# Layer norms in an attention and mixture-of-experts kernel: centring and scaling in one VectorE instruction, the mean copied to single precision by GpSimd

## The reference

```python
def _layernorm(x, axis=-1, eps=1e-05):
    m = jnp.mean(x, axis=axis, keepdims=True)
    v = jnp.var(x, axis=axis, keepdims=True)
    return (x - m) / jnp.sqrt(v + eps)
...
x = x + _layernorm(_L0_attn_ref(_layernorm(x), wq, bq, wk, bk, wv, bv, wo, bo))
x = x + _layernorm(_L0_ffn_ref(_layernorm(x), Ws, bs, Wg, Wu, Wd))
```

## Time and profile before

| what | value |
|---|---|
| median of 3 runs | 1080.92 us (1080.68 to 1082.11) |
| the profiled execution | 1085.77 us, span of the instructions 1084.0 us |
| TensorE busy | 839.0 us (77% of the span) |
| VectorE busy | 687.1 us (63%), 2640 instructions |
| ScalarE busy | 555.2 us (51%) |
| GpSimd busy | 367.8 us (34%), 427 instructions |
| mean granted TensorE clock | 0.695 of full speed |

### The profile page before, as it was taken

The page is one execution under the profiler, slowest core; times in us unless marked ns, Lnnn a source line. Parts: engine busy times, 40 slices in busy tenths (PEclk is TensorE's granted clock), DMA queues, the critical chain, the costliest instruction groups (busy, mean ns, idle before and its releaser), DMA issues. The chain is left out here.

```text
span 1084.0 us, 22600 instructions
## 1 busy us (share of the span) xinstructions
PE 839.0 (77%) x6684; PEld 494.9 (46%) x6685; DVE 687.1 (63%) x2640; ACT 555.2 (51%) x1006; POOL 367.8 (34%) x427
## 2 busy tenths in 40 slices
PE   4568687689878898788876059999999999999500
PEld 1123233234333333333333047787877877877400
DVE  5655676877877878778765525555555555555365
ACT  4677676655545455555544025545454454544244
POOL 3554644552442424325155411122112211221124
PEclk9555555555655555555555579999999999999855
DMA  4423222200010100001001141111011111110077
GB/s 146 133 87 114 80 88 72 63 21 20 22 30 11 40 2 26 25 1 41 1 21 36 36 141 36 44 44 44 29 44 44 41 32 44 44 44 31 28 233 232
DMA packets 52753, 61.44 MB, mean 57 GB/s; under 512 B 5264, under 2 KB 39696, under 8 KB 52688
## 3 DMA queue, kind: packets, MB, share of 16 engines
q1 hardware_dynamic: 46896, 46.14, 14.4%
q0 software_dynamic: 5792, 14.49, 3.7%
HBM read 37.71 MB, written 22.90 MB: 56 GB/s over the span
## 5 line engine op out<-in xcount | busy, mean ns | idle before, releaser
L552 ACT ACTIVATE pT<-bank 128x512 f16<-128x512 f32 (+1 forms) x384 | 194.8, 528 | 188.4 <-PE bank L909 186.2
L661 DVE CUSTOM_DVE_ANT_0 unused<-bank,mask 128x384 f16<-128x384 f32 (+3 forms) x512 | 232.4, 485 | 50.5 <-PE bank L900 46.2
L900 PE MATMUL bank<-kT,qT 32*128 32x384 f16 (+3 forms) x512 | 179.2, 448 | 49.3 <-DVE nmax L661 42.0
L1355 PE MATMUL bank<-xT,gu_part 128*128 128x256 f16 (+1 forms) x1716 | 201.3, 275 | 5.0 <-issue 4.2
L909 PE MATMUL bank<-qT,kT 32*128 32x384 f16 (+3 forms) x512 | 170.1, 440 | 24.5 <-ACT pT L552 23.7
L1355 PEld LDWEIGHTS bank<-xT,gu_part 128*128 (+1 forms) x1716 | 166.7, 100 | 39.6 <-issue 13.8
L1203 POOL DMA_INDIRECT expert_rows<-y_sb,dest x78 | 75.0, 962 | 320.0 <-DVE y_sb L1315 308.1
L1377 PE MATMUL bank<-wd_part,h 128*128 (+1 forms) x1404 | 171.7, 273 | 3.5 <-ACT h L1236 0.9
L450 POOL TENSOR_SCALAR_AFFINE_SELECT pT<-pT 128x512 f16<-128x512 f16 x128 | 80.5, 641 | 255.2 <-ACT pT L552 254.3
L1377 PEld LDWEIGHTS bank<-wd_part,h 128*128 128x128 f16 (+1 forms) x1404 | 126.4, 97 | 39.1 <-issue 17.9
L1296 DVE SCALAR_TENSOR_TENSOR hid<-bank,act_g 128x512 f32<-128x512 f32 (+2 forms) x156 | 86.7, 556 | 70.6 <-ACT act_g L1229 69.3
(11 more groups left out here) (148 smaller groups left out, 962.4 us busy)
## 6 DMA issues: line engine op xcount, KB each, us to landing
ys<-expert_rows SPq DMA_DIRECT2D x16, 512.0 KB, 4.8
stage<-wg SPq DMA_DIRECT2D x8, 688.0 KB, 4.1
stage<-wu SPq DMA_DIRECT2D x8, 688.0 KB, 4.1
stage<-wd SPq DMA_DIRECT2D x8, 640.0 KB, 4.3
xin<-dispatch_rows SPq DMA_DIRECT2D x39, 130.0 KB
out<-res SPq DMA_DIRECT2D x16, 256.0 KB, 3.2
x_sb<-x SPq DMA_DIRECT2D x8, 256.0 KB, 3.3
xr_sb<-x SPq DMA_DIRECT2D x8, 256.0 KB, 3.1
```

The lines of the kernel that those rows point to most:

```text
L552: sc.activation(pT[:, lo:hi], ST_BANK[i % 2][:, 0:hi - lo], ACT.Exp, scale=1.0 / INV_SCALE).then_inc(p_ready, 1)
L661: last = v.tensor_tensor_reduce(out=unused[:, i % 2, at:at + n], in0=S_BANK[i % 2][:, at:at + n], in1=mask[:, T - n:T], scale=-1.0, scalar ...
L900: last = mm(S_BANK[i % 2][:, at:at + n], qT[32 * j:32 * j + 32, g, P * qt:P * (qt + 1)], kT[32 * j:32 * j + 32, g, 0:n], start=True, stop= ...
L1355: last = mm(dst[0:width, :], gu_part[part][:, bass.ds(col + (k * GU + at), width)], xT[j][:, k, :], start=(s == 0), stop=(s == 2 * KD - 1))
```

## The change

A VectorE instruction can apply two operations with a scalar per partition each. The changed kernel subtracts the mean and multiplies by `rstd` in one instruction per tile; `cen` and the function `norm_centre` are gone. Both scalars are now of single precision, so GpSimd copies the four means from `mv` into a new tile `mean`, between `veps` and `std`. VectorE waits for `mean_ready` and `rstd_ready` at the place where it scaled before. In the tables the entries of the centring steps are dropped, and all other entries keep their group and step.

```diff
-        cen = sb(stack, "cen", [P, QT, D], F16)
+        mean = sb(stack, "mean", [P, QT], F32)
...
-        AT_NEXT_NORM = ((0, 0), (0, 1), (0, 2), (0, 3), (0, 4), (0, 6), (0, 7))
-        AT_FINISH = ((1, 4), (1, 6), (1, 7), (1, 8), (1, 9), (1, 10), (1, 10), (1, 11),
-                     (2, 0), (2, 1), (2, 2), (2, 3), (2, 4), (2, 5), (2, 6), (2, 7), (2, 10), (2, 11))
+        AT_NEXT_NORM = ((0, 0), (0, 1), (0, 2), (0, 6), (0, 7))
+        AT_FINISH = ((1, 4), (1, 6), (1, 7), (1, 8), (1, 9), (1, 10),
+                     (2, 0), (2, 1), (2, 2), (2, 3), (2, 4), (2, 5), (2, 10), (2, 11))
...
                     gp.tensor_scalar(veps[:, :], mv[:, :, 1], LN_EPS16, None, ALU.add).then_inc(veps_ready, 1)
+                    gp.tensor_copy(mean[:, :], mv[:, :, 0]).then_inc(mean_ready, 1)
                     pool.wait_ge(veps_ready, n + 1)
...
-                def norm_centre(src, n, half):
+                def norm_scale(dst, src, n, half):
                     if half == 0:
-                        dve.wait_ge(var_ready, n + 1)
-                    for t in HALVES[half]:
-                        last = v.tensor_scalar(cen[:, t, :], src[:, t, :], mv[:, t, 0:1], None, ALU.subtract)
-                    if half:
-                        last.then_inc(cen_ready, 1)
-
-                def norm_scale(dst, n, half):
-                    if half == 0:
-                        dve.wait_ge(cen_ready, n + 1)
+                        dve.wait_ge(mean_ready, n + 1)
                         dve.wait_ge(rstd_ready, n + 1)
                     for t in HALVES[half]:
-                        last = v.tensor_scalar(dst[:, t, :], cen[:, t, :], rstd[:, t:t + 1], None, ALU.mult)
+                        last = v.tensor_scalar(dst[:, t, :], src[:, t, :], mean[:, t:t + 1], rstd[:, t:t + 1],
+                                               ALU.subtract, ALU.mult)
                     return last
```

More of the change, by code:

```diff
@@ L226, in attention @@
         std_ready = sem("std_ready")
-        cen_ready = sem("cen_ready")
+        mean_ready = sem("mean_ready")
         rstd_ready = sem("rstd_ready")
@@ L709, in finish @@
                     elif at in (6, 7):
-                        norm_centre(y, n, at - 6)
-                    elif at in (8, 9):
-                        last = norm_scale(y, n, at - 8)
-                        if at == 9:
[L714 to L718, removed]
+                        last = norm_scale(y, y, n, at - 6)
+                        if at == 7:
+                            ch.mark(last)
+                    elif at == 8:
+                        add_x(b)
+                    elif at in (9, 10):
+                        if at == 9:
                             dve.wait_ge(x1_ready, b + 1)
-                        norm_stats(x1, at - 11)
-                    elif at == 13:
+                        norm_stats(x1, at - 9)
+                    elif at == 11:
                         norm_moments(n + 1)
[L723 to L726, removed]
+                    elif at in (12, 13):
+                        if at == 12:
                             dve.wait_ge(xn2_free, b + 1)
-                        last = norm_scale(xn2, n + 1, at - 16)
-                        if at == 17:
+                        last = norm_scale(xn2, x1, n + 1, at - 12)
+                        if at == 13:
                             last.then_inc(xn2_ready, 1)
@@ L802, in next_norm @@
                     elif at in (3, 4):
-                        norm_centre(x_sb, n, at - 3)
-                    elif at in (5, 6):
-                        if at == 5 and not first:
+                        if at == 3 and not first:
                             dve.wait_ge(xnT_mm, b)
-                        last = norm_scale(xn, n, at - 5)
-                        if at == 6:
+                        last = norm_scale(xn, x_sb, n, at - 3)
+                        if at == 4:
                             last.then_inc(xn_ready, 1)
```

## The result

The changed kernel takes 1082.56 us by the median of 12 runs (1081.14 to 1084.5), the kernel before 1080.42 on the same chip (12 runs, 1078.05 to 1082.11): a ratio of 1.0023, 95% interval 1.0015 to 1.0032. It is 2.1 us slower (the interval is 1.6 to 3.5 us); the forecast was 2.3. On a second chip, where both kernels take some 7 us longer, the ratio was 1.0013 (1.0000 to 1.0026), 1.3 us. The total agrees; the sum behind it agrees only in part.

What follows compares the result with a forecast made beforehand. No engine was taken as full: VectorE leads in a group's early steps, TensorE in steps 7 to 11, GpSimd where rstd is awaited. Gains 2.4, losses 4.7: 1080.92 + 2.3 = 1083.2 us, range 1078.4 to 1086.0.

Steps and rivals of the forecast that it cites:

- The fused instruction: VectorE scaling with two scalars: second scalar costs about 60 ns, 340 ns in all, 0.24 us a norm.
- The copy: GpSimd's cast of four means between veps and std: 0.15 us net wherever the wait for rstd or the cut counts.
- The input norms of batches 3 to 6: Group 0, steps 3 and 4: lost centrings gain 0.35 us a batch, longer scalings take back 0.10.
- The x1 norms: Group 2, steps 6 and 7, batches 2 to 6: TensorE's waits for maxima shrink, gaining 0.20 us a batch.
- Batch 7 and the close: Two norms each, scaling waiting for rstd: 0.60 us for the copy and 0.96 for the longer scalings.
- The norm of `y`: Removed centring worth 0; longer scalings cost 1.44 us over batches 1 to 6, the copy 0.30 over batches 2 to 6.
- The free second scalar: Rival: a fused VectorE instruction stays at 281 ns, giving 1080.2 us, no change; chance 0.30.
- the slow form: Rival: the fused VectorE instruction loses the fast rate, 540 ns instead of 281, giving 1095 us; chance 0.08.
- The disturbed centrings: Rival: centring pairs slowed beside GpSimd in batches 1 and 2 are real time, 4.3 us back, 1078.9 us; chance 0.10.

Runs made afterwards that it cites:

- one_scalar: Changed kernel with the mean's operand replaced by constant 0, one scalar per partition, copy kept: 1084.16 us, 0.9961 of the kernel before.
- y_early: Changed kernel with both halves of y's scaling in step 0 of group 2: 1079.90 us against 1080.91 for the kernel before, 0.9990.
- y_late: Changed kernel with the second half of y's scaling one step later, in step 2 of group 2: 1081.77 us, 1.0019 of the kernel before.
- after_again: The changed kernel once more, no edit, on another chip: 1088.84 us against 1087.51 for the kernel before, 1.0013.
- mv32: Changed kernel with mean and variance in single precision, read directly, no copy on GpSimd: 1088.37 us, 1.0006 of the kernel before.
- no_centre: Kernel before with the centring left out (mean not subtracted, no copy): 1082.53 us, 0.9947 of the kernel before.
- mv32_y_split: Changed kernel with y's norm in two steps as before, single-precision mean and variance, no copy: 1074.99 us, 0.9944 of the kernel before.
- best: mv32_y_split with one GpSimd pow instead of two for rstd: 1068.26 us, 0.9878 of the kernel before.

## Why the prediction came out right, point by point

- **The fused instruction** (340 ns forecast): 343, and `one_scalar` shows that the price is the second scalar's. Right, also where it counts: first norm 0.24 and, by `y_early`, 0.24 at each `y`.
- **The copy** (0.15 us net): mis-sized. The row has 187 ns, but the net is 0.06 in the first norm and some 0.03 in the others, because the forecast added the copy to the end of `veps`, and it overlaps it. First norm +0.27 and not +0.39; batches 0 to 2 +0.14 together and not +0.45 (within the spread of that stretch); at `y` the wait for `rstd` that was priced 0.30 didn't appear: `rstd` starts 0.52 us after `v` where it started 0.50 after, and the scaling has no wait. In the x1 norm of batch 1, with the cut, +0.18 came for 0.15.
- **The input norms of batches 3 to 6** (-0.35 and +0.10 each): -0.30. The step that failed is the +0.10: `xn` was not just in time. `one_scalar` has 8.30 without the second scalar, and TensorE is not idle before these transposes in either kernel.
- **The x1 norms** (-0.20 each): -0.20. Right in size. But the first centring pair there has 0.92 us in the earlier trace rows, not the undisturbed 0.48, since its second instruction met the cut, in all of the batches 2 to 6. The kernel before already had such meetings, and the prediction's own rows showed one.
- **Batch 7 and the close** (+1.56): +0.18. Both terms were too big, the copy's for the reason above. The scalings were taken to stand on the path in full, four times 0.24: the stretch at `y` at the close has that (1.82 to 2.06), the x1 norm there has 0.09, `y` in batch 7 has 0.04, and the x1 norm of batch 7 gets 0.19 shorter.
- **The norm of `y`** (+1.74 over six batches): +4.0, the term that was mis-sized most. The step said that each half is 0.12 us longer and no more; it did not ask which GpSimd instruction starts next. Before, the last of the four scalings began 0.21 us ahead of the cut (373.56 and 373.77). Three fused instructions ahead of it, each 0.06 us longer, bring it to 0.03 us ahead (372.91 and 372.94), and it waits. That is 0.42 us in each of six batches, 2.5 us.
- **The rivals.** The free second scalar fell by its rows, the slow form by the same. The disturbed centrings fell too: the wait for `rstd` in batch 1 went from 1.79 to 4.37 us, TensorE's for `xn` stayed at 1.75, and batches 1 and 2 gained nothing.

```profile
130.82 1.14 DVE L632 TENSOR_SCALAR xn<-x_sb,mean,rstd 128x256 f16<-128x256 f16 x2 [4.37 <-POOL rstd L432]
...
134.92 1.03 PE L863 MATMUL bank<-ident,xn 128*128 128x128 f16 x8 [1.75 <-DVE xn L632]
```

So 2.3 forecast and 2.1 measured is a sum in which a collision of 2.5 us that was missing stands against 2.3 us of terms that were too large (2.3 forecast, 2.5 more and 2.3 less: the 2.5 of the table). The places and the price of the second scalar were right; the largest single cost, the collision at `y`, was not in the forecast. The agreement to 0.2 us is luck.

## What to carry to other kernels

VectorE time that is taken out beside a wait comes back as a longer wait: 22.6 us of it were worth 2.2 to 2.4 here, nearly all at the two places where TensorE stood for the maxima. When an instruction gets longer, look in the trace for what starts next on the engine that shares its port with it: 0.18 us of delay decided on 0.42, and moving one entry of a table by a step took the 0.42 back. And the longest wait (`rstd`, 31 us before and 43 after) said what to shorten: the chain on four elements, not the work on 256.

## What the runs showed of the hardware

**Scalars per partition.** In SBUF with 16-bit data at 256 elements: one scalar 282 ns, two 343, two operations with one scalar 282. The fast rate is kept with two single-precision scalars.

**A cut and VectorE.** The slow instruction at `y` in the changed kernel, an undisturbed one in `y_late`, one that begins a little further ahead of a cut in the changed kernel, and a centring of the earlier trace rows in the kernel before (single rows of the timelines; the first two cuts are shown above, at 372.94 and at 373.58):

```profile
372.91 0.75 DVE L632 TENSOR_SCALAR y<-y,mean,rstd 128x256 f16<-128x256 f16 x1
```

```profile
373.98 0.34 DVE L632 TENSOR_SCALAR y<-y,mean,rstd 128x256 f16<-128x256 f16 x1
```

```profile
344.12 0.34 DVE L632 TENSOR_SCALAR xn<-x_sb,mean,rstd 128x256 f16<-128x256 f16 x1
344.23 0.74 POOL L451 TENSOR_SCALAR_AFFINE_SELECT pT<-pT 128x512 f16<-128x512 f16 x1 [1.19 <-ACT pT L553]
```

```profile
379.46 0.72 DVE L630 TENSOR_SCALAR cen<-x,mv 128x256 f16<-128x256 f16 x1
379.46 0.64 POOL L450 TENSOR_SCALAR_AFFINE_SELECT pT<-pT 128x512 f16<-128x512 f16 x1 [5.05 <-ACT pT L552]
```

The first ends at 373.66, 0.08 us after its cut, and the last at 380.18, also 0.08 us after its cut. That holds in all 14 traces: 141 centrings and scalings began between 0.07 us ahead of a cut and 0.39 us into it and met that cut alone, and each of them ended 0.08 us after the cut did, with one scalar or with two. The one in `y_late` begins 0.40 us into the cut and would end 0.09 us after it anyway, so it isn't delayed. An instruction that begins 0.10 to 0.12 us ahead keeps its length, and the cut is the one that gets longer (0.72 to 0.74 us for 0.64 beside a fused instruction, 0.67 to 0.68 beside one with one scalar). One that begins 0.17 us or more ahead, as the 0.21 of the kernel before, changes neither. So by the rows of VectorE the border lies between 0.07 and 0.10 us ahead of the cut. By the Trainium skill, "SBUF — State Buffer", section on the two separate sides, whoever starts first holds the shared ports for its whole instruction; the trace agrees, with either engine as the one that waits.

**Fewer instructions.** The Trainium skill, "VectorE: DVE Perf Modes", section with rules for kernel authors, advises for chained operations not to fuse for speed, and to keep the number of operations small. Here 96 fewer are 2.1 us slower, and the 2.2 us of the input and x1 norms are gained only where VectorE leads.

**TensorE's clock.** In the attention stage there are short stretches at the 2.4 GHz level (the profiler's granted clock is above 0.50 of full speed in the mean there), and their number differs between executions of one kernel. Two like stretches of the changed kernel, from the x1 transposes to the next `stats` (windows; columns as in the earlier trace rows):

```profile
321.07:337.42 16.35, 14.80 (x139) 6.93 (x139) 12.07 (x76) 10.12 (x20) 2.54 (x4) 0.58 0.01 2
386.76:404.32 17.56, 16.04 (x139) 7.11 (x139) 13.12 (x78) 10.17 (x20) 2.49 (x4) 0.50 0.01 1
```

The same 139 matmuls take 1.21 us less where the granted clock is 0.58 in the mean instead of 0.50, so part of the stretch was at the higher level. An execution has some more or fewer of these, which is as much as the whole change: the changed kernel has two of 16.35 us among the four after the x1 transposes of batches 2 to 5, and none in `after_again`. From the x1 transposes of batch 6 to the `att` transposes of batch 7, where no norm stands, `mv32`, `no_centre`, `mv32_y_split` and `best` have 27.0 to 27.1 us, most others 28.3. These four are the kernels that fuse and have no copy; no run shows why. In `mv32` all four of the stretches have 16.35 us in the profiled execution of 1079.93 us, 8.4 below the median of that kernel.

This is why sums were made from stretches, and not from the two spans, which say the reverse of the medians (1080.0 us for the changed kernel, 1084.0 for the kernel before). The attention part, up to the last transposes of `rows`, takes 608.5 us in the changed kernel and 607.5 in the kernel before. The rest, which the change leaves alone, takes 471.6 and 476.5. It has 476.4 to 478.0 us in the four traces from the second chip and 470.9 to 472.3 in all the others but that of the kernel before; the cause is open.
